# Twelve-step root chain run once for two tiles, gate and up products as three fp32r products, and the order of every engine laid out anew

## The reference

```
def attn_layer(x, Wqkv, qs, ksc, Wo):            # 16 heads of 64
    q, k, v = split(x @ Wqkv)
    q, k = l2norm(q) * qs, l2norm(k) * ksc
    q = q * cos * scale + rotate_half(q) * sin * scale
    k = k * cos / scale + rotate_half(k) * sin / scale
    return local_attention(q, k, v) @ Wo         # windows of 32, each sees itself and the one before
def ffn_layer(x, g, bln, W1, b1, W2, b2):        # W1 is 128 x 682, W2 341 x 128
    xn = (x - mean) / sqrt(var + 1e-5) * g + bln
    a, gate = split(xn @ W1 + b1)
    return a * gelu(gate) @ W2 + b2
for i in range(6):
    x = attn_layer(shift_tokens(x), ...) + x
    x = ffn_layer(shift_tokens(x), ...) + x
```

## Time and profile before

| | us |
|---|---|
| median of 3 runs | 4148.47 (4144.48 to 4149.37) |
| the profiled execution | 4148.09 |
| its span, first to last instruction | 4146.3 |
| PE busy | 3788.5 (91%) |
| POOL busy | 2942.9 (71%) |
| DVE busy | 2900.7 (70%) |
| ACT busy | 2376.3 (57%) |
| DMA queue q1 | 13.3% of 16 engines' span |

### The profile page before, as it was taken

One profiled execution on the slowest core, in us unless ns is written; L12 is line 12 of the kernel. 1 busy time (PEld: TensorE's weight loads), 2 busy tenths in 40 slices (PEclk: granted clock), 3 DMA queues, 4 the chain that ended last, 5 costly groups with the idle time before them and its releaser, 6 DMA issues.

```text
span 4146.3 us, 150150 instructions
## 1 busy us (share of the span) xinstructions
PE 3788.5 (91%) x64432; PEld 2730.8 (66%) x64432; DVE 2900.7 (70%) x5136; ACT 2376.3 (57%) x4221; POOL 2942.9 (71%) x4274
## 2 busy tenths in 40 slices
PE   6888899769999899998999989999899998999997
PEld 3444444357777677776777767777677776777774
DVE  3566655556777777777777777777777777777772
ACT  3322221146667667676666667776667766676662
POOL 0222222378888788887888878888788887888772
PEclk9999999879999999999999999999999999999998
DMA  1000000011111111111111111111111111111110
GB/s 67 3 6 6 6 3 3 16 47 39 38 36 41 46 45 41 38 39 41 48 42 37 40 39 49 42 38 40 40 44 46 39 37 44 42 48 41 40 36 25
DMA packets 96279, 147.03 MB, mean 35 GB/s; under 512 B 27264, under 2 KB 35840, under 8 KB 95488
## 3 DMA queue, kind: packets, MB, share of 16 engines
q1 hardware_dynamic: 95616, 137.42, 13.3%
HBM read 32.46 MB, written 4.19 MB: 9 GB/s over the span
## 4 chain that ended last, share of the span: by engine, by line
PE 80%; DVE 5%; POOL 5%; issue 4%; ACT 4%; DMA 1%; SPq 0%; POOLq 0%; ACTq 0%; DVEq 0%
PE bank L445 18%; PE bank L528 8%; PE bank L517 8%; PE bank L490 6%; PE bank L378 5%; PE bank L465 5%; PE bank L455 4%; PE bank L501 4%; PE bank L585 3%; PE bank L575 3%; PE bank L567 3%; PE bank L393 2%; PE bank L477 1%; POOL m L1341 1%; PE bank L420 1%
## 5 line engine op out<-in xcount | busy, mean ns | idle before, releaser
L445 PE MATMUL bank<-wqkv,xs 128*128 128x512 f32 x3456 | 1123.0, 441 | 18.2 <-DVE m L834 15.7
L1341 POOL TENSOR_TENSOR m<-m 128x512 f32<-128x512 f32 x768 | 969.2, 1283 | 67.8 <-DVE m L834 67.8
L445 PEld LDWEIGHTS bank<-wqkv,xs 128*128 128x128 f32 x3456 | 598.9, 194 | 161.7 <-issue 79.4
L832 DVE TENSOR_TENSOR m<-bank,tab 128x512 f32<-128x512 f32 x768 | 522.0, 680 | 216.3 <-ACT sq L1106 190.3
L1106 ACT ACTIVATE sq<-bank 128x512 f32<-128x512 f32 x768 | 456.4, 594 | 161.3 <-DVE ss L844 78.8
L834 DVE TENSOR_TENSOR m<-bank,tab 128x512 f32<-128x512 f32 x768 | 523.3, 681 | 18.5 <-POOL m L1341 18.5
L844 DVE TENSOR_REDUCE ss<-sq 128x8 f32<-128x512 f32 x768 | 503.4, 677 | 5.9 <-ACT sq L1106 5.1
L1349 POOL TENSOR_TENSOR S<-S,nw 128x1024 f32<-128x1024 f32 x192 | 365.3, 1902 | 193.2 <-DVE S L864 193.1
L517 PEld LDWEIGHTS bank<-P,big 64*64 64x64 f32 x24576 | 376.1, 135 | 97.7 <-issue 96.9
L1357 POOL TENSOR_TENSOR S<-S,rs 128x512 f32<-128x512 f32 x384 | 393.1, 1045 | 23.5 <-DVE rs L878 23.5
L1335 POOL TENSOR_TENSOR m<-m,nw 128x512 f32<-128x512 f32 x384 | 395.4, 1051 | 11.4
(11 more groups left out here) (202 smaller groups left out, 6600.7 us busy)
## 6 DMA issues: line engine op xcount, KB each, us to landing
big<-vst SPq DMA_DIRECT2D x1536, 64.0 KB, 2.0
stage<-in_wqkv SPq DMA_DIRECT2D x36, 256.0 KB, 3.0
tab<-in_tab SPq DMA_DIRECT2D x48, 128.0 KB, 2.3
big<-in_wa SPq DMA_DIRECT2D x1, 3460.0 KB, 12.5
wo<-in_wo SPq DMA_DIRECT2D x6, 512.0 KB, 3.7
big<-in_x SPq DMA_DIRECT2D x8, 256.0 KB, 3.2
keep<-Xr SPq DMA_DIRECT2D x8, 256.0 KB, 2.0
stage<-keep SPq DMA_DIRECT2D x8, 256.0 KB, 3.0
```

What stands on the lines that cost most here:

```text
L445: m = eng.matmul(pb[:, :], xt[a], wqkv[:, z, 512 * part:512 * part + 512], start=(n == 0), stop=(n == 2))
L832: eng.tensor_tensor(m1[:, part, :].rearrange("p (h d) -> p h d", d=DH), pv, ct.unsqueeze(1).to_broadcast([P, 8, DH]), ALU.mult)
L1341: eng.tensor_tensor(m1[:, part, :], m1[:, part, :], m2[:, part % 2, :], ALU.add).then_inc(s["g_add"], 1)
```

## The change

There are four parts.

1. **Roots.** `chain` runs in odd rounds only and takes the sums of two tiles at once: 64 columns of head sums and 8 of layer norms, 72 in all. `ss` and `nw` grow, a second buffer `mk1` takes the rotated keys of odd tiles, and what needs the roots moves one tile later: `turn_k`, `mask` and `sim` to n-2, `probs` and `values` to n-4, `out_proj` to n-5, the feed-forward by one unit.
2. **Gate and up.** ScalarE rounds `xn` to fp32r (`xn_high`), VectorE writes the remainder (`xn_low`); once per layer both do the same for W1. Each gate and up product is then three fp32r products into one bank.
3. **Orders.** The loops of all five engines are written anew, and `RING` gives some steps the other of the banks 2 and 3.
4. **Memory.** The scratch kept for GpSimd's own DMAs is set to 2048 bytes; the kernel has no such DMA, since every issue is SP's.

```diff
-RING = {... "v": (2, 2), "spread": 3, "gate": (2, 3, 3), "up": (2, 3, 2), ...}
+RING = {... "v": (2, 3), "spread": 2, "gate": (2, 3, 2), "up": (2, 3, 3), ...}
-    return STEPS * (g + 1 if g < NG else NG + (g - NG) // 4 + 1)
+    return STEPS * (g // 2 + 1 if g < NG else NG // 2 + (g - NG) // 4 + 1)
...
             def gate(u, f):
-                pe.wait_ge("a_xn", u + 1)
-                pe.wait_ge("d_ffn", 16 * (u // NC + 1))
+                pe.wait_ge("v_xl", u + 1)
+                pe.wait_ge("v_w1", u // NC + 1)
-                eng.matmul(pb[0:rows, :], w1[...], xn[:, :], start=True, stop=True)
+                for n, (z, a) in enumerate(((0, 0), (0, 1), (1, 0))):
+                    m = eng.matmul(pb[0:rows, :], w1r[:, z, at], xnr[:, a, :], start=(n == 0), stop=(n == 2))
...
+            def xn_low(u):                                   # vector
+                dv.wait_ge("a_xh", u + 1)
+                dv.wait_ge("p_fa", 3 * u)
+                eng.tensor_tensor(xnr[:, 1, :], xn[:, :], xnr[:, 0, :], ALU.subtract)
+                if u % NC == 0:
+                    eng.tensor_tensor(w1r[:, 1, :], w1, w1r[:, 0, :], ALU.subtract)
+            def xn_high(u):                                  # scalar
+                ac.wait_ge("a_xn", u + 1)
+                eng.activation(xnr[:, 0, :], xn[:, :], ACT.Copy, scale=1.0, bias=0.0)
+                if u % NC == 0:
+                    eng.activation(w1r[:, 0, :], w1, ACT.Copy, scale=1.0, bias=0.0)
...
             def chain(g):
-                if not 0 <= g < ROUNDS or g >= NG and g % 4:
+                if not 0 <= g < ROUNDS or g % 2 == 0 or g >= NG and g % 4 == 1:
                     return
                 if g < NG:
                     po.wait_ge("v_ss", 4 * g + 4)
-                    po.wait_ge("g_scl", 2 * (g - 1))
-                    po.wait_ge("g_sub", g - 1)
+                    po.wait_ge("g_scl", 2 * (g - 3))
+                    po.wait_ge("g_sub", g - 3)
...
-                scale(n - 1, 0)                              # gpsimd's loop
-                scale(n - 1, 1)
+                weighed(n - 3)
+                scale(n - 2, 0)
+                scale(n - 2, 1)
                 add(n, 0)
                 add(n, 1)
-                divide(n - 2, 0)
-                divide(n - 2, 1)
+                divide(n - 3, 0)
+                divide(n - 3, 1)
+                if q4 == 3:
+                    tables(u + 1)
                 add(n, 2)
                 add(n, 3)
-                weighed(n - 1)
                 chain(n)
```

More of the change, by code:

```diff
@@ L27 @@
 TURN = (0, 1, 4, 2, 3, 5)
-RING = {"tk": (3, 2), "tq": (3, 2), "pr": (3, 2), "v": (2, 2), "wo": 3,
-        "centre": 3, "variance": 2, "spread": 3, "gate": (2, 3, 3), "up": (2, 3, 2),
+RING = {"tk": (3, 2), "tq": (3, 2), "pr": (3, 2), "v": (2, 3), "wo": 3,
+        "centre": 3, "variance": 2, "spread": 2, "gate": (2, 3, 2), "up": (2, 3, 3),
         "down": 2}
@@ L247, in _ @@
             eng.dma_start(w2, w2_d[0]).then_inc(s["d_down"], 16)
-            for n in range(NG + 28):
+            for n in range(NG + 32):
                 u, i = n // 4, n % 4
@@ L574, in up @@
                 pb = claim(b)
-                eng.matmul(pb[0:rows, :], w1[:, 128 * f:128 * f + rows], xn[:, :], start=True, stop=True).then_inc(s["p_fa"], 1)
+                at = slice(128 * f, 128 * f + rows)
+                for n, (z, a) in enumerate(((0, 0), (0, 1), (1, 0))):
+                    m = eng.matmul(pb[0:rows, :], w1r[:, z, at], xnr[:, a, :], start=(n == 0), stop=(n == 2))
+                m.then_inc(s["p_fa"], 1)
                 vacant[b] = [("v_h", 3 * u + f + 1)]
@@ L622, in _ @@
                 proj(n, 0)
[L623 to L647 removed]
+                probs(n - 4, 0)
+                proj(n, 1)
+                probs(n - 4, 1)
+                out_proj(n - 5)
+                if q4 == 3:
+                    down(u - 4)
+                if q4 == 2:
+                    up(u - 4, 0)
+                    up(u - 4, 1)
+                if q4 == 1:
+                    gate(u - 4, 0)
+                    gate(u - 4, 1)
+                if q4 == 3:
+                    centre(u - 2)
+                    end_centre(u - 5)
+                values(n - 4)
+                proj(n, 4)
+                if q4 == 2:
+                    up(u - 4, 2)
+                proj(n, 2)
+                if q4 == 2:
+                    spread(u - 3)
+                    end_spread(u - 6)
+                turn_k(n - 2, 0)
+                proj(n, 3)
+                turn_k(n - 2, 1)
+                mask(n - 2)
+                proj(n, 5)
+                if q4 == 3:
+                    variance(u - 2)
+                    end_variance(u - 5)
+                if q4 == 1:
+                    gate(u - 4, 2)
+                sim(n - 2)
                 turn_q(n, 0)
[L649 to L650 removed]
                 turn_q(n, 1)
[L652 to L658 removed]
         @block.vector
@@ L900, in norm_step @@
                 dv.wait_ge("p_lnv", u + 1)
-                dv.wait_ge("g_ch", rooted(4 * u + 4))
-                eng.tensor_scalar(ss[:, 0, 32:36], bank[RING["variance"]][:, 0:4], 1e-5, None, ALU.add).then_inc(s["v_ln"], 1)
+                dv.wait_ge("g_ch", rooted(4 * u + 7))
+                eng.tensor_scalar(ss[:, 1, 64:68], bank[RING["variance"]][:, 0:4], 1e-5, None, ALU.add).then_inc(s["v_ln"], 1)
             def normed(u):
@@ L939, in end_step @@
                 dv.wait_ge("p_ev", k + 1)
-                dv.wait_ge("g_ch", rooted(4 * u + 16))
-                eng.tensor_scalar(ss[:, 0, 36:40], bank[RING["variance"]][:, 0:4], 1e-5, None, ALU.add).then_inc(s["v_e"], 1)
+                dv.wait_ge("g_ch", rooted(4 * u + 19))
+                eng.tensor_scalar(ss[:, 1, 68:72], bank[RING["variance"]][:, 0:4], 1e-5, None, ALU.add).then_inc(s["v_e"], 1)
             def ended(u):
```

221 lines of the change are left out of this document (106 added, 115 removed).

## The result

| us | before | after |
|---|---|---|
| median, 4 runs each | 4148.92 (4144.48 to 4149.52) | 3984.56 (3981.16 to 3987.72) |
| the profiled execution, its span | 4148.09, 4146.3 | 3984.39, 3982.6 |
| PE busy | 3788.5 (91%) | 3698.1 (93%) |
| POOL busy | 2942.9 (71%) | 2734.3 (69%) |
| clock granted over the span | 0.961 | 0.972 |

The ratio is 0.9613 with an interval of 0.9595 to 0.9630: 164 us less. The forecast was 135 less, 4013 us.

What follows compares the result with a forecast made beforehand. PE was taken to bound the kernel, POOL close behind. 4148.1 less 132 (48 units), less 15 (layers' ends), plus 12 (deeper pipeline) gave 4013 us; range 3965 to 4100, the forecast's own 3965 to 4050.

Steps and rivals of the forecast that it cites:

- What bounds: In the layers nearly all of the chain is PE; a regular unit goes from 64.94 to 62.2 us.
- Products: Gate and up: 288 products go from 0.86 to 0.70 us each, 46 us less, straight on the path.
- The wait at `centre`: PE's wait of about 1.1 us per unit behind `centre`, for bank 3 that ScalarE reads twice first, goes.
- 1.1 us of "issue" kept and 0.9 us for new waits: Per unit, the unexplained "issue" inside `sim` stays at 1.1 us; tight waits and changes between unlike products add 0.9.
- The clock: Time at 1.2 GHz, within 1.6 us of smaller things per unit; most behind `centre` goes with that wait.
- Roots for two tiles: GpSimd's root chain takes 4.9 us, twice per unit; POOL loses 6.4 us of work, by itself saving nothing.
- The rival of a late GpSimd: Everything behind the long chain waits if it passes about 6 us; 4219 us, slower; chance 0.07.
- some tenths at the gates: Behind ScalarE's four GELU and exp changes, at most some tenths of a us of waiting at the gates.
- Copies for the fp32r products: 48 copies on ScalarE and 48 subtractions on VectorE, and six each for W1, put nothing on the path.
- Layers' ends: At five layer boundaries, 3 us less each, 15 us in all, bounds 0 and 25.
- what PE can do meanwhile: At layers' ends, while staged weights are awaited, PE does `variance`, one more transpose and a projection, 1.3 us more.
- Deeper pipeline: One more unit's feed-forward falls behind the last projection, plus a little at the start: 12 us more, bounds 3 and 25.

Runs made afterwards that it cites:

- e2: The changed kernel with fp32 gate and up products again, without the copies for them; 4025.4 us, ratio 0.9724 to the kernel before.
- c1: The kernel before with only `centre` and `centred` moved to the start of the round, as in the change; 4127.3 us, ratio 0.9961.
- e1: The kernel before with fp32r gate and up products and the copies they need, old order kept; 4130.7 us, ratio 0.9971.
- e4: The kernel before with one operation in place of the twelve of GpSimd's root chain in odd rounds (wrong roots there); 4129.9 us, ratio 0.9971.
- d1: The changed kernel with twelve spare GpSimd operations in rounds with q4 = 0 only, right ahead of the GELU round; 4127.9 us, ratio 0.9970.
- c2: The kernel before with `centre` and `centred` moved early, and also `variance` ahead of `sim` and `norm_step` ahead of `largest`; 4163.9 us, ratio 1.0040.
- f1: The kernel before with fp32r gate and up products and one operation for the twelve-step root chain in odd rounds; 4125.5 us, ratio 0.9957.
- e3: The changed kernel with twelve spare dependent GpSimd operations of 40 columns in every even round; 4144.5 us, ratio 1.0001 to the kernel before.
- d2: The changed kernel with twelve spare GpSimd operations in rounds with q4 = 2 only; 3994.3 us, ratio 0.9651 to the kernel before.

## Why the prediction was right, and where it was not

- **What bounds.** Right. The regular unit was to come to 62.2 us, at most 63; it is 61.1 from `down` to `down` and 61.75 as a mean with the units at a lower clock.
- **Products**, 46 us: right in the order they were forecast for, 41 by `e2` and 0.70 to 0.71 in the chain. As a price by itself, wrong: 13 us in the old order.
- **The wait at `centre`**, 1.1 us per unit: gone. The bank's next claim by `turn_k` has no wait, as worked out. The 106.6 us of the earlier trace rows, which I gave to the units, are 38 waits of 1.3 us, 48.6 in all, and five of 11.2 to 12.1 at the layers' ends. Closing that hole alone (`c1`) brings 14 of the 53 us, since `variance` and `probs` then wait in its place.
- **1.1 us of "issue" kept and 0.9 us for new waits**: too much together. Work by the sum is 60.2 us and the unit 61.1 to 61.75. "Nothing in the change touches it" was wrong of the pieces inside `sim`: PE's waits there fell from 24.2 to 5.3 us. Of the 0.83 us of "issue" left in a regular unit's chain 0.12 are in `sim` and 0.41 are the wait for Wo. A unit became 3.08 us shorter and not 2.75, which is 16 us in 48.
- **The clock.** The 16 us are in size within this term too. I had it inside 1.6 us of smaller things. The dips of the regular units stood nearly all behind the hole at `centre`: the `out_proj` behind it took 2.3 us or more in 19 of the 41 rounds outside the layers' ends (2.75 in the earlier trace rows; in `e1` 21 of 41), and in none of the changed kernel. Over the whole span 328 us passed at 1.2 GHz before and 226 after, which is what clocks of 0.961 and 0.972 come to. PE does in 102 us at 1.2 GHz what takes 51 at 2.4, so up to 51 of the 164 are this.
- **Roots for two tiles.** The size was right, 4.6 us for 4.9. "By itself this saves nothing" was near: 14 us in `e4`, where the waits of `turn_k` for `scale` are 6 us less on PE and 9 less on its loads. What I didn't see is that the new order cannot do without it. The rival of a late GpSimd named the right way (`weighed`, `exps`, ScalarE's list), but put its decision at a chain of 6 us, by the margin of `turn_k`. The margin that gives way first is that of the bank that GELU reads, in the q4 = 1 round: I had it as "some tenths at the gates". `d1` shows 3.9 us of extra work there as 3.0 us per unit, 134 us more than the same work in another round.
- **Copies for the fp32r products.** "Nothing on the path" held: no PE wait on `xnr` or `w1r` stands in the list. (The prediction prices a copy and a subtraction at 1.3 us in one place and at 1.6 in another, which moves the sum by 1 us.)
- **Layers' ends**, -15: measured -9. The step that failed is "what PE can do meanwhile": I followed PE and ScalarE to bank 3 and missed `turn_q`'s claim of bank 2 and the norm's place in VectorE's list. By its words the prediction is wrong if a new wait of over 40 us stands among PE's. One does, at 54.7 us; but it stands at the layers' ends, not at `turn_k` or a transpose behind GELU, and is what is left of the old wait there (the earlier trace rows has its longest at 12.1, this one 11.4).
- **Deeper pipeline**, +12: the remainder is -7, the difference of three larger numbers. The tail is there, `down` to `down` 3943.25 to 3959.14, 15.9 us, for 14.9, and from `out_proj` of round 192 to the end it is 116.0 us for 91.1, so 25 more. Against it the stretch up to the first layer's end is about 21 us shorter than the gain per unit and boundary explains, in part by the feed-forward that moved out of it, and the eight units of the last layer cost 13.6 us above regular ones, for 23.9. I had priced neither the second at its full size nor the third at all. No experiment took this term apart.

Against the forecast of -132 - 15 + 12 = -135 the sum reads -148 - 9 - 7 = -164: the three terms were off by 16, 6 and 19 us, the second the other way. What stays open: how the 164 divide. Single edits of the old order bring 13, 14 and 14 us, two of them together 16, `centre`, `variance` and the norm's step moved together -14 (slower), and the whole change 164. So no part has a price of its own, and shares can be told only as what is lost when one is taken from the whole: 41 for the products, 160 for GpSimd's even rounds without a chain (4144.5 - 3984.6). That closing one or two of the holes brings little, and that the new order needs the shorter chain, is shown by `e1`, `c1`, `c2`, `f1`, `e3` and `d1`; which of the many moves of order the rest of the gain needs is not shown. That the clock makes the last hole so dear is read from durations behind waits and was not tested by itself. The "issue" pieces in `sim` have no cause that the trace shows, neither for being there nor for having shrunk.

## What to carry to other kernels

When an engine's list has several short holes, don't price the closing of each by its wait and add up: ask of each what the next claimant is, since the first hole is the cover of the second. Here edits that bring 13 or 14 us each by themselves are parts of a change that brings 164. An engine's busy share doesn't tell what relief on it is worth; look at the way with the least room that passes through it, and at the round in which it does (`d1` against `d2`). For a kernel that loads weights between stages, follow every bank that is claimed there, to its reader's place in the reader's own list, and every load to the step that needs it: an "issue" piece can be a wait for a DMA, as at `out_proj` here.

## What the runs showed of the hardware that was not expected

- A wait of 1.3 us in PE's list, the same in nearly every regular unit, is followed by records at 1.2 GHz in 19 of 41 units and not in the others: 16 products of `out_proj` in 2.3 to 3.6 us for 1.79. With the changed kernel the granted clock of the window went from 0.97 to 0.99.
- Three fp32r products of 512 columns take 0.70 us and one fp32 product 0.86, 0.81 of it and not three quarters.
- The change of ScalarE's function table for GELU takes 1.28 us. In the changed kernel it begins at 2040.98, when the first gate is there, and is not in the chain outside the tail; in `e3` it begins right behind a late `exps` and is in the chain 41 times with all of its 1.28 us.
- Twelve dependent steps on GpSimd cost 4.0 us at 40 columns and 4.6 at 72: 80% more columns for 15% more time. Each step ends 0.08 us before the next one begins.
